# Graph kernel on one core: wide blocks of sweeps 3 and 4 as seven products, degrees by columns in sweep 1 and by rows in sweep 2

## The reference, cut to what matters

```python
    h = jnp.maximum(_layernorm(x, axis=-1), 0.0)
    x = x + _L0_gnn_ref(h, adj, L0_gnn_W)        # twice: agg = adj @ x; x = tanh(concat([agg, x]) @ W[k])
    h = jnp.maximum(_layernorm(x, axis=-1), 0.0)
    x = x + _L1_gnn_ref(h, adj, L1_gnn_weight, L1_gnn_bias)   # adj @ (x @ weight) + bias
    h = jnp.maximum(_layernorm(x, axis=-1), 0.0)
    x = x + _L2_gnn_ref(h, adj, L2_gnn_u)        # adj @ (x * (u >= 0.1) / 0.9)
    h = jnp.maximum(_layernorm(x, axis=-1), 0.0)
    x = x + _L3_gnn_ref(h, adj, L3_gnn_W)        # [x, adj @ x / (sum(adj, axis=1) + 1)] @ W.T
```

## Time and profile before

| | |
|---|---|
| median of three runs | 2263.71 us |
| span of the profiled execution | 2260.8 us |
| TensorE busy in it | 2230.8 us (99%) |
| VectorE busy | 1356.8 us (60%) |
| ScalarE busy | 118.7 us (5%) |
| `adj` and the rest, read by DMA | 822.31 MB, 365 GB/s over the span |
| granted TensorE clock, mean | 0.999 |
| the chain that ended last | TensorE 94%, VectorE 3%, DMA 2% of the span |

### The profile page before, as it was taken

The page is one execution under the profiler, slowest core; times in us unless marked ns, Lnnn a source line. Parts: engine busy times, 40 slices in busy tenths (PEclk is TensorE's granted clock), DMA queues, the critical chain, the costliest instruction groups (busy, mean ns, idle before and its releaser), DMA issues.

```text
span 2260.8 us, 33750 instructions
## 1 busy us (share of the span) xinstructions
PE 2230.8 (99%) x14246; PEld 1093.6 (48%) x14246; DVE 1356.8 (60%) x2804; ACT 118.7 (5%) x246; POOL 9.6 (0%) x22
## 2 busy tenths in 40 slices
PE   6999999999999999999999999999999999999999
PEld 3555555555555434455454444444444444444446
DVE  7677666624777395765889888877534322222226
ACT  1000000000002210101100000000001000000000
POOL 0000000000000000000000000000000000000000
PEclk9999999999999999999999999999999999999999
DMA  9999999999999878889888888886999999999998
GB/s 397 421 417 400 417 404 389 391 384 396 398 410 372 295 287 305 317 319 324 355 315 332 320 316 324 316 343 251 345 376 405 408 410 406 410 407 406 406 406 324
DMA packets 117014, 826.62 MB, mean 366 GB/s; under 512 B 13824, under 2 KB 16128, under 8 KB 16896
## 3 DMA queue, kind: packets, MB, share of 16 engines
q1 hardware_dynamic: 112752, 820.04, 92.0%
q0 software_dynamic: 768, 2.10, 0.3%
q10 hardware_dynamic: 3344, 2.33, 0.3%
HBM read 822.31 MB, written 2.10 MB: 365 GB/s over the span
## 4 chain that ended last, share of the span: by engine, by line
PE 94%; DVE 3%; DMA 2%; issue 0%; SPq 0%; ACT 0%; DVEq 0%
PE double_acc L836 52%; PE single_acc L808 17%; PE spare L836 14%; PE spare L808 6%; DMA ring<-in_adj 2%; PE spare L866 2%; PE single_acc L866 2%; PE natural L930 1%; DVE deg_part L1112 1%; DVE deg_part L1111 1%; DVE stack L1150 0%; DVE centred L1075 0%; DVE deg_part L1108 0%; DVE stats L1063 0%; DVE held L1212 0%
## 5 line engine op out<-in xcount | busy, mean ns | idle before, releaser
L836 PE MATMUL double_acc<-ring,operand 128*64 128x512 f32 x5696 | 1252.2, 593 | 0.2 <-DVE operand L1349 0.2
L836 PEld LDWEIGHTS double_acc<-ring,operand 128*64 128x64 f32 x5696 | 455.3, 137 | 702.0 <-issue 684.6
L808 PE MATMUL single_acc<-ring,operand 128*64 128x256 f32 x3472 | 410.7, 381 | 21.1 <-DVE operand L1089 11.9
L808 PEld LDWEIGHTS single_acc<-ring,operand 128*64 128x64 f32 x3472 | 277.9, 137 | 171.4 <-issue 75.9
L836 PE MATMUL spare<-ring,operand 128*64 128x512 f32 x1456 | 330.3, 592 | 0.6 <-DMA ring<-in_adj 0.6
L1131 DVE TENSOR_TENSOR partial<-spare,partial 64x256 f32<-64x256 f32 (+1 forms) x200 | 105.3, 526 | 360.6 <-PE spare L808 218.0
L1112 DVE TENSOR_TENSOR deg_part<-deg_part,ring 128x1024 f32<-128x1024 f32 x216 | 264.6, 1225 | 7.4
L1111 DVE TENSOR_TENSOR deg_part<-deg_part,ring 128x1024 f32<-128x1024 f32 x216 | 264.0, 1222 | 4.7
L836 PEld LDWEIGHTS spare<-ring,operand 128*64 128x64 f32 x1456 | 125.7, 137 | 149.2 <-issue 141.5
L1131 DVE TENSOR_TENSOR partial<-single_acc,partial 64x256 f32<-64x256 f32 x122 | 51.5, 422 | 176.7 <-PE single_acc L808 174.6
L808 PE MATMUL spare<-ring,operand 128*64 128x256 f32 x1152 | 134.3, 379 | 0.0
(11 more groups left out here) (110 smaller groups left out, 965.7 us busy)
## 6 DMA issues: line engine op xcount, KB each, us to landing
ring<-in_adj SPq DMA_DIRECT2D x766, 1024.0 KB, 7.5
held<-in_adj SPq DMA_DIRECT2D x12, 1024.0 KB, 10.6
kept<-in_adj SPq DMA_DIRECT2D x2, 1024.0 KB, 11.7
for_layer<-in_u POOLq DMA_DIRECT2D x16, 128.0 KB, 2.4
out_rows<-resid ACTq DMA_DIRECT2D x15, 128.0 KB, 7.0
resid<-in_x SPq DMA_DIRECT2D x2, 512.0 KB, 6.0
resid<-in_x SPq DMA_DIRECT2D x1, 1024.0 KB, 13.5
out_rows<-resid ACTq DMA_DIRECT2D x2, 64.0 KB, 1.7
```

Of the source, the lines that this page charges most:

```text
L808: last = nc.tensor.matmul(acc[half_of(h), 0:HALF], operand[:, b.j * TPB + t, half_of(b.row.half)], stream[:, t, nodes_of(h)], start=b.firs ...
L836: last = nc.tensor.matmul(acc[half_of(half), :], operand[:, b.j * TPB + t, half_of(half)], stream[:, t, :], start=b.first and t == 0, stop ...
```

## The change

- The seven-product scheme leaves sweep 2 and goes to sweeps 3 and 4: every row with more than 7 wide blocks does all of them so but the first three, the sixth and the last: 3, 4, ... 10 blocks in the rows 8 to 15 of sweep 3, the same in the rows 7 to 0 of sweep 4, 104 in all. The row's first two `sums7` are made at once after `mixed` of the row before (or, in the first such row, after its first block). The results always lie in `single_acc`, so late groups of these rows have only `spare0` and `spare1`.
- `make_sums` has three operations instead of four: the first two are one of 1024 values per partition.
- The degrees: in sweep 1 each block on or below the diagonal is added to a 512-wide sum of its row in `store` (`add_lower`, one add of 1024 and two of 512), where the 16 row sums of `below` stand; in sweep 2 each wide block is added (`add_upper`, two adds of 1024). Sweep 3 adds none.
- One store of 13 slots takes the place of ring, held and kept. Five of them are shared with the degree sums and the block sums and open to loads only after the last seven-product block; until then 8 are in use. A block is used again only within 12 blocks, so there are 795 loads and not 780; three of the fifteen come from the row 15 that was retained for sweep 5.
- The diagonal blocks (2, i, i) of rows 0 to 5 move from sweep 1 to sweep 2.

```diff
-SEVEN_SWEEP = 2
-SEVENS = {6: 3, 5: 4, 4: 5, 3: 6, 2: 6, 1: 6}
...
+SHARED = 5
 RING = 8
+SLOTS = SHARED + RING
...
+REUSED_WITHIN = 12
+UPPER_SWEEP = 2
+SEVEN_SWEEPS = (3, 4)
+SEVENS_OVER = 7
+PLAIN_FIRST = 3
+SEVENS_BEFORE_PLAIN = 2
+SUMS = 2
...
+        if self.sweep in SEVEN_SWEEPS and len(self.double) > SEVENS_OVER:
+            first, end = PLAIN_FIRST, len(self.double) - PLAIN_END.get((self.sweep, i), 1)
+            between = first + SEVENS_BEFORE_PLAIN
+            self.sevens = [j for n, j in enumerate(self.double) if first <= n < end and n != between]
...
+        if row.sweep == 2 and row.i not in FILL_UP[2] or row.sweep == 3 and row.i and row.i not in FILL_DOWN:
+            at[1].append(lambda: late(row.sweep, row.i, [row.i]))
...
+        if what == "mixed" and of.r + 1 in firsts:
+            out.extend(("sums7", b) for b in firsts[of.r + 1])
+        elif what == "block" and of.kind == "double" and of.first and of.row in rows and of.row.r - 1 not in firsts:
+            out.extend(("sums7", b) for b in firsts[of.row.r])
...
+LOWER_BLOCKS = [b for b in BLOCKS if b.row.sweep == 1 and b.kind != "late" and b.j <= b.row.i]
+UPPER_BLOCKS = [b for b in BLOCKS if b.row.sweep == UPPER_SWEEP and b.kind == "double"]
...
+    opened = max(b.number for b in BLOCKS if b.seven)
+    free = {slot: -1 if slot >= SHARED else opened for slot in range(SLOTS)}
...
+                nc.vector.tensor_tensor(deg_part[:, :], data[:, 0:2 * BLOCK], data[:, 2 * BLOCK:], ALU.add).then_inc(deg_added, 1)
+                dve.wait_ge(deg_added, n + 1)
+                to = below(b.row.i)
+                    link(nc.vector.tensor_tensor(to, to, deg_part[:, 0:BLOCK], ALU.add))
+                    link(nc.vector.tensor_tensor(to, to, deg_part[:, BLOCK:], ALU.add))
+                if b is mine[-1]:
+                    fold(0, b.row.i, to)
...
-                link(nc.vector.tensor_tensor(t1, y12, y11, ALU.subtract))
-                nc.vector.tensor_tensor(y12, y22, y12, ALU.subtract)
+                link(nc.vector.tensor_tensor(t1_t3, y12_y22, y11_y12, ALU.subtract))
                 link(nc.vector.tensor_tensor(t2, y22, t1, ALU.subtract))
                 nc.vector.tensor_tensor(t4, y21, t2, ALU.subtract).then_inc(sums_made, 1)
```

More of the change, by code:

```diff
@@ L246, in downwards @@
     def downwards(row):
[L248 to L249 removed]
+        if row.sweep == 3 and row.i >= 1 and row.i - 1 not in FILL_UP[4] and row.i - 1 not in TURN:
+            late(4, row.i - 1, [row.i - 1])
     for row in ROWS[:NB]:
@@ L385, in with_sevens @@
-    return steps
+        steps.append((what, of))
+        if what == "post" and (of.sweep, of.i) in columns:
+            steps.append(("combine", of))
+        elif what == "block" and of.seven:
+            n = every.index(of)
+            of_row = [b for b in every if b.row is of.row]
+            if of is of_row[-1]:
+                steps.append(("mix", of.row))
+            following = every[n + SUMS:n + SUMS + 1]
+            if of is not of_row[-1] and following and following[0].row is of.row:
+                steps.append(("sums7", following[0]))
+        elif of in rows and what == ("post" if of.r % NB == NB - 1 else "doubles"):
+            steps.append(("mixed", of))
@@ L413, with degree_group, __init__ @@
+def degree_group(row):
+    return [*DEGREES_AT].index(row.i)
 class Load:
[L416 to L417 removed]
+    def __init__(self, first):
+        self.uses, self.slot, self.turn = [first], None, None
 def make_loads():
[L422 removed]
+    loads, of, latest = [], [], {}
     for b in BLOCKS:
[L424 to L432 removed]
+        at = b.row.i, b.j
+        load = latest.get(at)
+        near = load and b.number - load.uses[-1].number <= REUSED_WITHIN
+        if load and not load.uses[0].seven and (near or b.row.sweep == SWEEPS and at in RETAINED):
@@ L528, in make_places @@
         if what == "block" and of.kind == "single" and of.first:
-            singles[SINGLE[of.row.r % 2]].append((n, ("single", of.row)))
-    taken = {of.r: n for n, (what, of) in enumerate(PLAN) if what == "first"}
+            singles[SINGLE[of.row.r % 2]].append((n, of.row.r))
+        elif what == "block" and of.seven and of.j == of.row.sevens[0]:
+            for bank in SINGLE:
+                singles[bank].append((n, of.row.r))
+    taken = {of.r: n for n, (what, of) in enumerate(PLAN) if what == "first" and not of.sevens or what == "mixed"}
     place_of, before, last, first = {}, {}, {}, None
@@ L541, in make_places @@
                 choices = SPARE + [bank for bank in SINGLE
-                                   if all(taken[row.r] < first if at < first else at > n + IDLE_FOR for at, (_, row) in singles[bank])]
+                                   if all(taken[r] < first if at < first else at > n + IDLE_FOR for at, r in singles[bank])]
         elif what == "turn" and turned_by_tensor(of) or what == "degree":
@@ L1001, in _ @@
             for what, row in PLAN:
-                if what in ("block", "added", "added_both", "combine", "sums7", "mixed"):
+                if what in ("block", "added", "added_both", "combine", "sums7", "mixed", "degree"):
                     continue
@@ L1234, in mix @@
                 n = SEVEN_ROWS.index(row)
-                sums, both = seven[n % 2]
-                mine, other = half_of(1), half_of(0)
+                mine = half_of(row.half)
                 wait_stack(row)
```

342 lines of the change are left out of this document (156 added, 186 removed).

## The result

The changed kernel takes **2343.42 us** (median of four runs, 2342.42 to 2344.38), the kernel before 2263.72 beside it (2263.48 to 2263.84). The ratio is 1.0354 with a 95% interval of 1.0341 to 1.0367: 3.5% slower. The forecast was 2313 with a range of 2266 to 2334. The direction was right, the size was not: the loss over the span of before is 79.7 us where 49.6 had been counted.

The account below looks back on a forecast made before the run. TensorE was taken as the bound, busy 2230.8 of 2260.8 us. 2260.8 - 30.4 (shorter blocks) + 32 (degrees) + 42 (sweep 4 row starts) + 3 (DMA) + 3 (small terms) = 2310.4, plus 2.9 to the median: 2313 us, range 2266 to 2334.

Parts of the forecast that it names:

- The prices of blocks: On TensorE: a wide block 3.43 us, a single one 1.72, one of seven products 3.02, so 0.41 saved a block.
- The degree term: End of sweep 1 and rows 14 to 8 of sweep 2: VectorE's degree work holds up TensorE, 32 us (24 to 38).
- Sweep 3 cost nothing: Sweep 3: VectorE loses the degrees and gets less work in block sums; costed at nothing, far end 12 us.
- the sweep 4 term: Row starts of sweep 4: block sums waiting for a load stand ahead of `finish` in VectorE's queue, 42 us.
- rivals 1 and 2: First: only the degrees bite, sweep 4 loses under 1 us a row, 2273 us, 0.15. Second: scheme pays, 2239 us, 0.09.
- Rival 3: More than counted: sweep 3 waits (12), landings of 10 us in sweep 4, DMA-bound last stretch (12); up to 2352 us, 0.12.
- The start of each row of sweep 4: TensorE waits at the third late group: 5.4 us for seven rows, 4.1 for row 0, 42 us in all.
- the wait is the landing time less 2.4: Row starts of sweep 4: TensorE's wait follows from when the second seven-product block's load lands, 8.0 us after issue.
- at the change from sweep 3 to 4 ... 2 us: Small term: at the change from sweep 3 to 4 `mixed` and its wait lie on the chain, 2 us.
- I take 3 us: Last stretch: four blocks more are loaded, 10 us of DMA, partly hidden; 3 us, ends 0 and 12.
- The far end of 12 us: Upper end of the 3 us counted for four more loaded blocks in the last stretch.
- can't be had while the run lasts: Seven-product blocks alternating with single ones: two loads take 4.99 us at 420 GB/s against 4.75, so 0.24 of 0.41 is lost.

Follow-up runs that it names:

- runs 2 and 3: Kernel after with 44 and with 22 useless matmuls, respectively, ahead of each of the eight late groups of sweep 4 that waited: 2356.41 and 2327.85 us.
- run 6: Kernel after with the four additions out of the single accumulator's banks ahead of `finish` also for row 15 of sweep 3 and row 0 of sweep 4: 2333.89 us.
- run 1: Kernel after with `finish` ahead of the next row's block sums in sweep 4: 2302.63 us, ratio 1.0173 to the kernel before.
- run 12: 35 seven-product blocks added late in rows 7 to 1 of sweep 4, against a version with 65 in sweep 3 alone (2261.18 us): 2265.55 us.
- run 2: Kernel after with 44 useless matmuls ahead of each of the eight late groups of sweep 4 that waited: 2356.41 us.

## Why the prediction was wrong in size

**Right, with its numbers.** The prices of blocks. The degree term (32 counted, 33.9 measured), row by row: the takings of rows 13, 14 and 15 of sweep 1, which answer to the earlier trace rows, and of rows 14, 13, 12 and 11 of sweep 2:
```profile
648.65 0.68 DVE L1335 TENSOR_TENSOR stack<-double_acc,stack 64x512 f32<-64x512 f32 x1
666.32 0.68 DVE L1335 TENSOR_TENSOR stack<-double_acc,stack 64x512 f32<-64x512 f32 x1
680.68 0.68 DVE L1335 TENSOR_TENSOR stack<-double_acc,stack 64x512 f32<-64x512 f32 x1
695.04 0.68 DVE L1335 TENSOR_TENSOR stack<-double_acc,stack 64x512 f32<-64x512 f32 x1
716.97 0.69 DVE L1335 TENSOR_TENSOR stack<-double_acc,partial 64x512 f32<-64x512 f32 x1
732.99 0.69 DVE L1335 TENSOR_TENSOR stack<-double_acc,partial 64x512 f32<-64x512 f32 x1
750.30 0.69 DVE L1335 TENSOR_TENSOR stack<-double_acc,partial 64x512 f32<-64x512 f32 x1
...
767.84 0.69 DVE L1335 TENSOR_TENSOR stack<-double_acc,partial 64x512 f32<-64x512 f32 x1
```
Rows 13, 14, 15 of sweep 1: 17.67, 14.36, 14.36 (counted 17.8, 14.5, 14.4). Then 21.93, 16.02, 17.31, 17.54 (20.2, 15.6, 17.2, 17.5). Sweep 3 cost nothing, as counted. The mechanism and the place of the sweep 4 term were right too, and rivals 1 and 2 are out. Rival 3, more than counted, had the direction and the region (2333 to 2352), but of its three terms only the later landings came, and in part.

**Wrong: "The start of each row of sweep 4", 42 us, measured 63.** The step "the wait is the landing time less 2.4" held: loads landed later than the 8.0 us of the earlier trace rows,
```profile
store<-in_adj SPq DMA_DIRECT2D x53, 1024.0 KB, 9.1
```
and the eight waits sum to 48.4. What failed is that a wait was priced at its own length. TensorE comes out of it at half clock, and the block behind takes on average 5.0 and not 3.4 us: 12.7 us more in the eight rows (runs 2 and 3). The last 1.9 us of the 63 are small losses elsewhere in those rows.

**Wrong: "at the change from sweep 3 to 4 ... 2 us" and "I take 3 us" for the last stretch.** 7.3 and 12.0. For the last stretch the forecast took DMA for the limit and did not ask what frees the bank that the next block writes. It was `mixed`, at both places behind `finish` (run 6). The far end of 12 us had the right size by chance, for another reason.

**Missing on the other side:** 7.3 us of waits that before had and after has not. The largest of them, 4.07 us, stands in the view of waits of the kernel before. The forecast's 2313 with the measured sizes put in is 2313 + 1.9 - 7.3 + 5.3 + 21.0 + 9.0 = 2343.

**DMA.** The prediction said that 0.24 of the 0.41 us "can't be had while the run lasts" and counted nothing for it, as the waits leave time to catch up. In the kernel after that held. Once the waits are taken out it no longer does: in run 1 20 us came back as later waits, and run 12 gained nothing. The Trainium skill's DMA: Bandwidth & Descriptors, Where 436 GB/s comes from, has some 358 GB/s as what HBM gives a core; here it is again not the limit, with 421 GB/s shown in a stretch of 5 us and over 100 us in run 12.

## What to carry to other kernels

An operation that waits for a load must not stand ahead of one on which the next row depends; look at what is behind it in the same queue, and at what frees each bank. A faster block pays only where its loads have room too: read the DMA share of that stretch before the TensorE share. Price a wait of TensorE by its length and by the slow block behind it, and first list the waits that the old kernel has.

## What the runs showed of the hardware

- Behind waits of TensorE of 5.47 and 10.07 us the granted clock was 0.50 over the next 3.4 us of work: 16 records of a matmul of 256 columns in 3.40 us, not 1.73. At the posts it is seen in their duration: 1.12 us behind waits of 3.07, 4.07 and 5.08, and 0.69 behind one of 1.35. Work that fills the wait keeps 1.00: the run with 22 useless matmuls in each of eight waits was 15.6 us faster than the one without.
- A float32 matmul of 128 columns by 128x64 costs 0.22 us (two records of 0.11) in a row of 44; a block's 256 columns cost as much (1.73 / 16 = 0.11 a record). In that row of run 2 (2223.85 to 2233.50) the weight loads were busy for 9.65 of 9.65 us, so they may be what sets the pace; no run tests it.
- This program on one core draws 420 to 421 GB/s over stretches of 5, 40 and 100 us (the end of sweep 5 in the kernel after, the start of the kernel before, 2100 to 2200 us of run 12). Other stretches of 90 and 100 us with a DMA share of 1.00 to 1.01 ran at 405 to 416.
